# Two-tensor forms for VectorE's 128x4 passes, a wait ahead of three input loads and new instruction lists in a gated cross-attention and quantised feed-forward kernel

## The chip, the cores and the metric

The kernel runs on one core of one Trainium2 chip. Its time is the device time of one launch in microseconds (us), the median of the runs shown. The core has five engines that run their own instruction lists and wait for each other by semaphores: TensorE (PE; its weight loads are PEld), VectorE (DVE), ScalarE (ACT), GpSimd (POOL) and SyncE (SP), which here only issues DMA transfers. ScalarE issues DMA transfers too, at the head of its list.

## The reference, cut to what matters

```python
x = x + tanh(g_xattn) * xattn(layernorm(x), ctx)        # x: 4 x 512 x 256, ctx: 4 x 64 x 256, 16 heads of 16
x = x + tanh(g_ffn) * ffn(layernorm(x))

def xattn(q, k, v):                                     # k = v = ctx
    qh, kh, vh = (q @ Wq.T + bq), (k @ Wk.T + bk), (v @ Wv.T + bv)
    return softmax(qh @ kh.T / 4) @ vh @ Wo.T + bo      # by head

def ffn(x):                                             # 256 -> 1024 -> 256
    h = bit_linear(x, w1)
    h = silu(depthwise_conv1d(h, conv_w, 3 taps) + conv_b)
    return bit_linear(h, w2)

def bit_linear(x, w):                                   # rows of x to 8 bits, w to -1, 0, 1
    s = 127 / max(max_abs(x, by row), 1e-5);  xq = round(x * s) / s
    t = 1 / max(mean_abs(w), 1e-5);           wq = clip(round(w * t), -1, 1) / t
    return xq @ wq.T
```

The norm is over the 256 columns, with 1e-5 added to the variance.

## The kernel before, in words

The four batches of 512 rows pass through one software pipeline. A batch stands in SBUF as four tiles of 128 rows, so each per-row number (mean, root, step) of a batch is a block of 128x4. The stages of batch b are:

- `statistics(b)` and `mean_variance(b)` on VectorE (L676 to L686): statistics by row, then two short passes, `var` = variance + 1e-5 (L685) and `minus_mean` (L686). GpSimd takes the root (`root`, L1378). `norm(b)` runs on VectorE for batch 0, on ScalarE for batch 1 (it then needs `shift`, the negated mean times the root), on GpSimd for 2 and 3.
- TensorE turns the normed rows (`turn_xn`), projects q, computes `scores` once for the row maxima (`row_max`, L720, VectorE) and a second time turned (`scores_t`), minus the maxima; ScalarE takes `exponentials`; TensorE does `values` (L358) and `denominators` (L369), and `project_o` (L397). `residual1` on VectorE adds x.
- `statistics2`, `mean_variance2`, `root2` and `norm2` repeat the norm on the new x. `scale1(b)` on VectorE finds the row maxima of 128x4 (L768) and makes the step (L774), its reciprocal (L777) and the factor back (L780). GpSimd quantises (`quantise1`), TensorE turns and multiplies in eight chunks (`hidden`, L436), and VectorE multiplies each chunk by the factor (`dequantise`, L790).
- The convolution of batches 0 to 2 is half on TensorE (`convolve`, L445) and half on ScalarE and GpSimd (`tap` on ScalarE, `add_left` and `add_right` on GpSimd, L1433 and L1440). Batch 3 is all on TensorE, its second half in two halves of 256 columns. ScalarE takes `silu`.
- VectorE takes the maxima of the hidden rows (`hidden_max_whole`, L812, 4.4 us), `scale2(b)` makes step (L833), reciprocal (L836) and factor (L837), and `quantise_hidden` (L860) writes the quantised tile; TensorE does the product with w2 (`second`, L507). The residual is added by ScalarE and GpSimd for batches 0 to 2, by VectorE for batch 3.

At the start SP issues x of batch 0, the q weights, x of batches 1, 2 and 3 and w2 (L254 to L259), one behind the other and without a wait. ScalarE issues nine more loads (L1202 to L1210): identity, small parameters, context, key weights, a pair indicator, value and output weights, bias rows, w1 and the convolution weights. ScalarE sums the absolute values of w1 and w2 (`weight_sum`, L1058); `weight_scales` turns the sums into scales; w1 is quantised by VectorE, w2 by GpSimd.

The order of the work is written out by hand: each engine has a flat list of calls with the PSUM bank that each uses and the marks that free the bank (from L512 for TensorE, L898 for VectorE, L1211 for ScalarE, L1462 for GpSimd). An engine does its list in order, so an instruction that waits holds all behind it.

Of the kernel before, what the change touches and what calls it, by code (L numbers as in the profile page):

```python
# [12 lines left out]
P = 128  # L13
# [4 lines left out]
T = N // P  # L18
# [33 lines left out]
SPLIT = 3  # L52

# [33 lines left out]
def build(nc, x, ctx_t, attn_w, w1_t, w2_t, conv_d, small, rows, ident, pair_ind, out):  # L87
# [3 lines left out]
    with ExitStack() as es:  # L91
# [29 lines left out]
        minus_half = sb("minus_half", [P, 1])  # L121

# [54 lines left out]

        staged = hid[:, 1].rearrange("p q n i -> p (q n i)")
# [24 lines left out]
        var_ready, rstd_ready = signal("var_ready", 2), signal("rstd_ready")  # L203
# [14 lines left out]
        var2_ready, rstd2_ready = signal("var2_ready", 2), signal("rstd2_ready")  # L218
# [14 lines left out]
        hq_ready = signal("hq_ready", T)  # L233
# [34 lines left out]
        def _(pe):  # L268
# [204 lines left out]
            def spread_scale2_half(b, a, bank, *free):  # L473
# [16 lines left out]
            def spread_scale2(b, bank, *free):  # L490
# [3 lines left out]
                for k in range(T):  # L494
                    last = nc.tensor.transpose(ps[:, bank, k * P:(k + 1) * P],
# [3 lines left out]
            def second(b, h, bank, *free):  # L499
# [4 lines left out]
                for k in (2 * h, 2 * h + 1):  # L504
                    pe.wait_ge(*hq_ready(b, k))
# [47 lines left out]
            project_q(3, 0, 1, mx_ready(1, 2))
            turn_max(1, 5, xT_ready(3, 1))
            project_o(0, 0, 4, oT_ready(0, 0))
            scores_t(1, 0, 6, mx_ready(1, 3))
            scores_t(1, 1, 2, mx_ready(2, 0))
            scores_t(1, 2, 4, x1_ready(0, 0), neg_ready(1))
            project_o(0, 1, 0, oT_ready(0, 1))
            values(1, 0, 6, p_ready(1, 0))  # L560
            denominators(1, 0, 7, p_ready(1, 0))
# [483 lines left out]
        def _(act):  # L1045
# [102 lines left out]
            def own_hid(b):  # L1148
# [4 lines left out]
                if b >= 2:  # L1153
                    act.wait_ge(*hq_ready(b - 2, T - 1))
# [417 lines left out]
```

## Time and profile before

| what | us |
| --- | --- |
| runs of the kernel before: median (lowest to highest) | 168.42 (167.06 to 169.79) |
| the profiled execution | 169.36 |
| span of its trace | 167.2 |

The rows below come from that one profiled execution. Its time is 2.16 us more than its span and 0.94 us more than the median. In a row "x4" is a count of instructions; "[1.69 <-DMA row<-rows]" is the time that the engine stood idle before it and what ended that.

### The profile page before, as it was taken

How to read it: one execution, taken by the hardware profiler on the slowest of the kernel's cores; microseconds unless marked ns; L12 is line 12 of the kernel's file. 1: busy time of each engine (PE TensorE's matmuls, PEld its weight loads, DVE VectorE, ACT ScalarE, POOL GpSimd, SP SyncE). 2: the span in 40 equal slices, each digit the busy share in tenths (PEclk: the TensorE clock that was granted, in tenths of full speed). 3: DMA queues.
4: the chain of work that ended last, by engine and by line, in shares of the span. 5: the costliest groups of instructions: out<-in, count | busy, mean ns of one | idle time of the engine just before them, and what ended most of it. 6: DMA issues, size and time to landing. Idle time of an engine off the chain costs nothing.

```text
span 167.2 us, 3548 instructions
## 1 busy us (share of the span) xinstructions
PE 143.8 (86%) x1314; PEld 79.1 (47%) x1324; DVE 135.2 (81%) x240; ACT 112.3 (67%) x176; POOL 88.3 (53%) x88
## 2 busy tenths in 40 slices
PE   7839979999799999999999796999565999984792
PEld 3238435424565336652576242568333353743461
DVE  6455999961953669995837999999999969989993
ACT  0304598779616488899999997999498586652220
POOL 0204899999910542398370089882979943200330
PEclk9996999999999999999999999999998799999999
DMA  4999800000000000000000000000030000110024
GB/s 134 269 386 395 339 6 0 4 0 0 0 0 2 4 0 0 0 0 4 4 2 0 4 0 2 0 6 0 0 125 0 4 4 0 67 67 0 3 79 169
DMA packets 5919, 8.68 MB, mean 52 GB/s; under 512 B 528, under 2 KB 4880, under 8 KB 5648
## 3 DMA queue, kind: packets, MB, share of 16 engines
q1 hardware_dynamic: 4608, 5.51, 9.6%
q10 hardware_dynamic: 1296, 2.97, 4.7%
q8 instruction: 10, 0.16, 0.4%
q14 instruction: 5, 0.04, 0.1%
HBM read 6.38 MB, written 2.10 MB: 51 GB/s over the span
## 4 chain that ended last, share of the span: by engine, by line
PE 29%; DVE 24%; ACT 24%; issue 15%; DMA 5%; ACTq 1%; DVEq 0%
ACT hid L1181 6%; DMA w_attn<-attn_w 5%; PE ps L445 5%; DVE u L790 4%; DVE mx L720 4%; ACT probs L1120 3%; PE ps L311 3%; DVE hid_q L860 3%; DVE hmax L812 3%; PE ps L348 3%; PE ps L507 2%; ACT side L1169 2%; ACT xn L1079 2%; PE ps L397 2%; DVE top L768 2%
## 5 line engine op out<-in xcount | busy, mean ns | idle before, releaser
L790 DVE TENSOR_TENSOR u<-ps,deq_b 128x512 f32<-128x512 f32 x32 | 20.2, 679 | 4.1 <-PE ps L436 3.6
L1433 POOL TENSOR_TENSOR hid<-hid,side 128x512 f32<-128x512 f32 x12 | 15.6, 1305 | 8.8 <-ACT side L1166 8.8
L720 DVE TENSOR_REDUCE mx<-ps 128x16 f32<-128x1024 f32 x16 | 18.8, 1212 | 1.4 <-PE ps L321 1.4
L445 PE MATMUL ps<-u,conv_w 32*32 32x512 f32 (+1 forms) x576 | 18.5, 544 | 0.9 <-ACT hid L1188 0.7
L1120 ACT ACTIVATE probs<-ps 128x1024 f32<-128x1024 f32 x16 | 15.4, 1029 | 5.6 <-PE ps L348 5.5
L1445 POOL TENSOR_TENSOR x_s<-x_s,grown 128x512 f32<-128x512 f32 x6 | 7.6, 1277 | 21.1 <-ACT grown L1198 21.1
L860 DVE TENSOR_TENSOR hid_q<-hid,ps 128x1024 f16<-128x1024 f32 x16 | 18.6, 1215 | 0.0
L436 PE MATMUL ps<-xqT,w1q 128*128 128x512 bf16 x57 | 15.3, 397 | 3.6 <-ACT xqT L1139 2.9
L1440 POOL TENSOR_TENSOR hid<-hid,side 128x512 f32<-128x512 f32 x12 | 15.5, 1305 | 4.2 <-ACT side L1169 3.8
L507 PE MATMUL ps<-w2q,hid_q 128*128 128x256 f16 x128 | 15.6, 273 | 1.3 <-DVE hid_q L860 1.3
L311 PE MATMUL ps<-xT,w_attn 128*128 128x512 f32 x32 | 15.0, 601 | 0.9 <-DVE mx L720 0.9
L1404 POOL TENSOR_TENSOR rstd<-var,minus_half 128x4 f32<-128x4 f32 x4 | 4.1, 1023 | 21.8 <-DVE minus_mean L762 21.8
L397 PE MATMUL ps<-w_attn,oT 128*128 128x256 f32 x64 | 14.9, 384 | 0.1
L507 PEld LDWEIGHTS ps<-w2q,hid_q 128*128 128x128 f16 x128 | 11.9, 98 | 5.4 <-issue 1.7
L397 PEld LDWEIGHTS ps<-w_attn,oT 128*128 128x128 f32 x64 | 11.8, 190 | 3.4 <-issue 1.6
L812 DVE TENSOR_REDUCE hmax<-hid 128x512 f32<-128x4096 f32 x3 | 13.2, 4409 | 0.2 <-ACT hid L1181 0.2
L445 PEld LDWEIGHTS ps<-u,conv_w 32*32 32x32 f32 x576 | 8.5, 105 | 8.9 <-issue 5.0
L1181 ACT ACTIVATE hid<-ps,par 128x512 f32<-128x512 f32 x16 | 10.3, 731 | 2.8 <-PE ps L445 2.7
L1161 ACT ACTIVATE hid<-u,par 128x512 f32<-128x512 f32 x12 | 9.5, 788 | 3.4 <-DVE u L790 3.4
L743 DVE SCALAR_TENSOR_TENSOR x_s<-ps,tg,x_s 128x512 f32<-128x512 f32 x8 | 5.9, 748 | 6.9 <-PE ps L397 6.8
L436 PEld LDWEIGHTS ps<-xqT,w1q 128*128 128x128 bf16 x64 | 5.9, 99 | 11.5 <-ACT xqT L1139 3.9
L1376 POOL TENSOR_TENSOR kbd<-kT,par 128x1024 f32<-128x1024 f32 x4 | 7.6, 1907 | 6.2 <-ACT kT L1052 6.2
(125 smaller groups left out, 307.2 us busy)
## 6 DMA issues: line engine op xcount, KB each, us to landing
x_s<-x SPq DMA_DIRECT2D x4, 512.0 KB, 12.2
out<-x_s SPq DMA_DIRECT2D x6, 256.0 KB, 2.1
hid<-w_t SPq DMA_DIRECT2D x1, 1024.0 KB, 18.4
hid<-w_t ACTq DMA_DIRECT2D x1, 1024.0 KB, 12.3
w_attn<-attn_w ACTq DMA_DIRECT2D x1, 512.0 KB, 10.0
out<-x_s SPq DMA_DIRECT2D x4, 128.0 KB, 1.8
conv_w<-conv_d ACTq DMA_DIRECT2D x1, 384.0 KB, 13.1
w_attn<-attn_w SPq DMA_DIRECT2D x1, 256.0 KB, 5.7
```

Of the source, the lines that this page charges most:

```text
L311: last = nc.tensor.matmul(ps[:, bank, :], w_attn[:, 0, c, m * P:(m + 1) * P], xT[:, c, :], start=(c == 0), stop=(c == DC - 1))
L397: last = nc.tensor.matmul(ps[:, bank, k % 2 * D:(k % 2 + 1) * D], oT[:, c, k * P:(k + 1) * P], w_attn[:, 3, c, :], start=(c == 0), stop=(c ...
L436: last = nc.tensor.matmul(ps[:, bank, :], w, xqT[:, b % 2, c, :], start=(c == 0), stop=(c == DC - 1))
L445: last = nc.tensor.matmul(ps[ROWS * g:ROWS * g + ROWS, banks[s], first:first + n], conv_w[rg, 4 * q + s, tap, :], u[rg, 4 * q + s, first + ...
L507: last = nc.tensor.matmul(ps[:, bank, k % 2 * D:(k % 2 + 1) * D], hid_q[:, f, k * P:(k + 1) * P], w2q[:, f, :], start=(f == 0), stop=(f == ...
L720: nc.vector.tensor_reduce(mx[:, b % 2, k, 0:HEADS], ps[:, bank:bank + 2, :].rearrange("p c (h k) -> p (c h) k", k=KEYS), AX.X, ALU.max).th ...
L790: nc.vector.tensor_tensor(u[:, f, 1:N + 1], ps[:, bank, :], deq1_b[:, b % 2, :], ALU.mult).then_inc(u_ready.sem, 1)
L812: nc.vector.tensor_reduce(hmax[:], hid[:, b % 2, 0:FP].rearrange("p q n i -> p n q i"), AX.XY, ALU.max, apply_absolute_value=True).then_in ...
L860: nc.vector.tensor_tensor(hid_q[:, :, tile].rearrange("p (q i) n -> p q i n", i=2), hid[:, b % 2, 0:FP, tile, :].rearrange("p q n i -> p q ...
L1120: nc.scalar.activation(probs[:, r], ps[:, bank:bank + 2, :], ACT.Exp, scale=SCORE_SCALE).then_inc(p_ready.sem, 1)
L1181: nc.scalar.activation(dst, src, ACT.Silu, bias=par[:, CB + f:CB + f + 1]).then_inc(hid_ready.sem, 1)
L1433: nc.gpsimd.tensor_tensor(dst, dst, side[:, m % TMPS, 0, :], ALU.add).then_inc(left_ready.sem, 1)
```

## The change

Three things change.

1. The 128x4 passes (and the 128x2 ones of batch 3) that had a number or a column as a scalar now have it as a second tensor, broadcast from a column in SBUF. Four columns are set for it at the start. `minus_mean` is computed only for the batches that ScalarE normalises; VectorE's and GpSimd's norm subtract the mean itself. GpSimd's root now waits for `var` alone.
2. SP waits for the key weights ahead of x of batch 1.
3. All four lists are written anew. Code for a variant in which GpSimd quantises one hidden tile is added, for the batches in TURNED, which is empty.

```diff
+TURNED = frozenset()
...
-                nc.vector.tensor_scalar(var[:, b], mv[:, b, :, 1], LN_EPS, None, ALU.add).then_inc(var_ready.sem, 1)
-                nc.vector.tensor_scalar(minus_mean[:, b], mv[:, b, :, 0], -1.0, None,
-                                        ALU.mult).then_inc(var_ready.sem, 1)
+                nc.vector.tensor_tensor(var[:, b], mv[:, b, :, 1], eps[:].to_broadcast([P, T]),
+                                        ALU.add).then_inc(var_ready.sem, 1)
+                if b in SCALED:
+                    nc.vector.tensor_tensor(minus_mean[:, b], mv[:, b, :, 0], minus_one[:].to_broadcast([P, T]),
+                                            ALU.mult).then_inc(mean_ready.sem, 1)
...
-                nc.vector.tensor_scalar(step1[:, a], top1[:, a], CLIP, 1.0 / QMAX, ALU.max,
-                                        ALU.mult).then_inc(step1_ready.sem, 1)
+                nc.vector.scalar_tensor_tensor(out=step1[:, a], in0=top1[:, a], scalar=CLIP,
+                                               in1=step_of[:, 0:1].to_broadcast([P, T]), op0=ALU.max,
+                                               op1=ALU.mult).then_inc(step1_ready.sem, 1)
...
-                nc.vector.tensor_scalar(deq1[:, a], step1[:, a], wmean[:, 0:1], None,
+                nc.vector.tensor_tensor(deq1[:, a], step1[:, a], wmean[:, 0:1].to_broadcast([P, T]),
                                         ALU.mult).then_inc(scale1_ready.sem, 1)
...
+            nc.vector.memset(eps[:], LN_EPS).then_inc(zeroed, 1)
+            nc.vector.memset(minus_one[:], -1.0).then_inc(zeroed, 1)
+            nc.vector.memset(step_of[:, 0:1], 1.0 / QMAX).then_inc(zeroed, 1)
+            nc.vector.memset(step_of[:, 1:2], 1.0 / (QMAX * F16_STEP)).then_inc(zeroed, 1)
...
             sp.dma_start(w_attn[:, 0], attn_w[:, 0]).then_inc(wq_in, 16)
+
+            sp.wait_ge(wk_in, 16)
             sp.dma_start(x_s[:, 1], x_v[1]).then_inc(x_ins[1], 16)
...
                 if b >= 2:
-                    act.wait_ge(*hq_ready(b - 2, T - 1))
+                    act.wait_ge(*hid_taken(b - 2, T - 2))
+                    act.wait_ge(*hid_taken(b - 2, T - 1))
...
             root(0)
             spread_keys(0)
+            spread_keys(1)
+            residual_base(0)
             root(1)
-            residual_base(0)
+            root(2)
+            root(3)
             residual_base(1)
-            root(2)
-            spread_keys(1)
```

`scale2`, `scale2_of_half` and `mean_variance2` change as `scale1` and `mean_variance` do. ScalarE's `take_q(0, 0)`, `weight_sum(0)`, `take_q(0, 1)`, `norm(1)`, `weight_sum(1)`, `take_xT(1)` now stand in this order; before it was `norm(1)`, both `take_q(0)`, both `take_xT(1)`, both `weight_sum`.

On VectorE, before the weights of the feed-forward are scaled, the list before reads (stat and mv are the statistics of a batch, mx its row maxima, wmean the weights' mean):

```order
L707 TENSOR_TENSOR vbd<-ps,row 64x2x8x16 x4
L676 BN_STATS stat<-x_s 128x6 x4
L682 BN_AGGR mv<-stat 128x2 x4
L685 TENSOR_SCALAR var<-mv 128x4
L686 TENSOR_SCALAR minus_mean<-mv 128x4
L720 TENSOR_REDUCE mx<-ps 128x16 x4
L676 BN_STATS stat<-x_s 128x6 x4
L877 TENSOR_SCALAR wmean<-ps 128x2
L881 RECIPROCAL wscale<-wmean 128x2
L882 TENSOR_SCALAR wdeq<-wmean,tg 128x1
L682 BN_AGGR mv<-stat 128x2 x4
```

The changed list reads at the same place:

```order
L726 TENSOR_TENSOR vbd<-ps,row 64x2x8x16 x4
L693 BN_STATS stat<-x_s 128x6 x8
L699 BN_AGGR mv<-stat 128x2 x4
L702 TENSOR_TENSOR var<-mv,eps 128x4
L699 BN_AGGR mv<-stat 128x2 x4
L702 TENSOR_TENSOR var<-mv,eps 128x4
L739 TENSOR_REDUCE mx<-ps 128x16 x4
L900 TENSOR_SCALAR wmean<-ps 128x2
```

The statistics of batch 3 (the second half of the x8) moved ahead of the four row maxima of batch 0.

On TensorE, around the output projection of batch 0 (w_attn<-oT) and the turned scores of batch 1 (neg_max with ind, then qT with kbd), the list before reads:

```order
L397 MATMUL ps<-w_attn,oT 128x256 x4
L344 MATMUL ps<-neg_max,ind 128x512 x2
L348 MATMUL ps<-qT,kbd 128x512 x2
L344 MATMUL ps<-neg_max,ind 128x512 x2
L348 MATMUL ps<-qT,kbd 128x512 x2
L344 MATMUL ps<-neg_max,ind 128x512 x2
L348 MATMUL ps<-qT,kbd 128x512 x2
L397 MATMUL ps<-w_attn,oT 128x256 x4
L358 MATMUL ps<-probs,vbd 32x512 x4
L369 MATMUL ps<-probs,ones_den 32x512 x4
L344 MATMUL ps<-neg_max,ind 128x512 x2
L348 MATMUL ps<-qT,kbd 128x512 x2
```

The changed list reads there:

```order
L412 MATMUL ps<-w_attn,oT 128x256 x8
L359 MATMUL ps<-neg_max,ind 128x512 x2
L363 MATMUL ps<-qT,kbd 128x512 x2
L359 MATMUL ps<-neg_max,ind 128x512 x2
L363 MATMUL ps<-qT,kbd 128x512 x2
L359 MATMUL ps<-neg_max,ind 128x512 x2
L363 MATMUL ps<-qT,kbd 128x512 x2
L359 MATMUL ps<-neg_max,ind 128x512 x2
L363 MATMUL ps<-qT,kbd 128x512 x2
L326 MATMUL ps<-xT,w_attn 128x512 x2
L384 MATMUL ps<-probs,ones_den 32x512 x4
L373 MATMUL ps<-probs,vbd 32x512 x4
```

The two halves of the projection stand together, the four turned scores behind them, and values and denominators of batch 1 after all four.

On TensorE near the end, around the hidden chunks of batch 3 (xqT with w1q; two of the x10 before the first of them belong to it too), the convolutions (u with conv_w) and the product with w2 (w2q with hid_q), the list before reads:

```order
L445 MATMUL ps<-u,conv_w 32x512 x48
L507 MATMUL ps<-w2q,hid_q 128x256 x16
L436 MATMUL ps<-xqT,w1q 128x512 x10
L445 MATMUL ps<-u,conv_w 32x512 x48
L436 MATMUL ps<-xqT,w1q 128x512 x2
L507 MATMUL ps<-w2q,hid_q 128x256 x16
```

The changed list reads there:

```order
L460 MATMUL ps<-u,conv_w 32x512 x48
L451 MATMUL ps<-xqT,w1q 128x512 x16
L460 MATMUL ps<-u,conv_w 32x512 x48
L460 MATMUL ps<-u,conv_w 32x256 x48
L524 MATMUL ps<-w2q,hid_q 128x256 x16
L503 MATMUL ps<-idf,hmax 128x128 x4
```

All eight chunks of batch 3 follow the convolution of batch 2 directly, and the product with w2 of batch 1 comes after the first half convolution of batch 3.

## Rows read from the trace of the kernel before

**Rows 1.** The page: busy us, share of the span and instructions of each engine.

```profile
PE 143.8 (86%) x1314; PEld 79.1 (47%) x1324; DVE 135.2 (81%) x240; ACT 112.3 (67%) x176; POOL 88.3 (53%) x88
```

**Rows 2.** Windows of 10 us: busy us of each engine, TensorE's clock, DMA share, GB/s.

```profile
10.00:20.00 10.00, 9.00 (x31) 6.67 (x32) 6.62 (x18) 3.42 (x7) 4.56 (x4) 0.83 1.03 395
...
70.00:80.00 10.00, 9.76 (x74) 4.37 (x75) 7.33 (x17) 10.00 (x16) 9.04 (x9) 1.00 0.01 2
...
90.00:100.00 10.00, 9.05 (x66) 3.66 (x70) 9.63 (x18) 9.97 (x14) 3.25 (x6) 1.00 0.01 2
...
150.00:160.00 10.00, 6.05 (x47) 4.17 (x46) 9.86 (x16) 2.73 (x8) 1.27 (x1) 1.00 0.07 26
```

**Rows 3.** The chain that ended last: start us, us on it, what.

```profile
2.14 8.72 DMA w_attn<-attn_w
...
20.95 2.28 DVE var L685
...
53.96 1.00 PE ps L358 x8
...
55.81 0.32 PE ps L344 x2
...
57.96 1.36 ACT xn L1079 x3
```

**Rows 4.** Short VectorE passes by line: ns shortest/median/longest, first and last start.

```profile
L685 DVE TENSOR_SCALAR var<-mv x4: 170/568/2283, 6.9 to 30.0; 128x4 f32<-128x4 f32 x4
...
L774 DVE TENSOR_SCALAR step<-top x4: 171/498/953, 61.3 to 123.3; 128x4 f32<-128x4 f32 x4
...
L780 DVE TENSOR_SCALAR deq<-step,wmean x4: 199/200/1120, 61.6 to 124.4; 128x4 f32<-128x4 f32 x4
...
L833 DVE TENSOR_SCALAR step<-top x3: 170/320/323, 98.6 to 147.5; 128x4 f32<-128x4 f32 x3
...
L837 DVE TENSOR_SCALAR deq<-step,wdeq x3: 200/327/409, 99.0 to 147.8; 128x4 f32<-128x4 f32 x3
```

**Rows 5.** Timelines of GpSimd and VectorE: start us, us, engine, line, what, count.

```profile
18.51 4.70 POOL L1399 TENSOR_TENSOR x_s<-x_s,bo_g 128x1024 f32<-128x1024 f32 x2
...
101.37 1.30 POOL L1440 TENSOR_TENSOR hid<-hid,side 128x512 f32<-128x512 f32 x1
...
101.87 0.82 DVE L774 TENSOR_SCALAR step<-top 128x4 f32<-128x4 f32 x1
102.73 0.18 DVE L777 RECIPROCAL qscale<-step 128x4 f32<-128x4 f32 x1
102.83 1.12 DVE L780 TENSOR_SCALAR deq<-step,wmean 128x4 f32<-128x4 f32 x1
```

**Rows 6.** Timelines of VectorE, ScalarE and SP, and one DMA issue (us to landing).

```profile
5.08 1.41 DVE L676 BATCH_NORM_STATS2 stat<-x_s 128x6 f32<-128x256 f32 x4 [0.87 <-DMA x_s<-x]
...
11.45 1.41 DVE L676 BATCH_NORM_STATS2 stat<-x_s 128x6 f32<-128x256 f32 x4 [1.66 <-DMA x_s<-x]
...
14.54 2.09 DVE L714 TENSOR_SCALAR bo_g<-row,tg 128x256 f32<-128x256 f32 x1 [1.69 <-DMA row<-rows]
...
24.57 1.91 ACT L1058 ACTIVATE w2q<-hid 128x2048 f16<-128x2048 f32 x1
...
59.93 1.25 ACT L1093 ACTIVATE qT<-ps,par 128x512 f32<-128x512 f32 x2
...
3.49 4.02 SPq L259 DMA_DIRECT2D hid<-w_t  x1
...
hid<-w_t SPq DMA_DIRECT2D x1, 1024.0 KB, 18.4
```

**Rows 7.** Timeline of VectorE in batch 3: start us, us, what, [idle before, releaser].

```profile
134.52 1.29 DVE L790 TENSOR_TENSOR u<-ps,deq_b 128x512 f32<-128x512 f32 x2 [0.41 <-PE ps L445]
...
136.70 3.08 DVE L790 TENSOR_TENSOR u<-ps,deq_b 128x512 f32<-128x512 f32 x5 [0.90 <-PE ps L436]
...
148.79 1.75 DVE L821 TENSOR_REDUCE hmax<-hid 128x256 f32<-128x1536 f32 x1 [0.77 <-ACT hid L1188]
```

More of the change, by code:

```diff
@@ L477, in spread_scale2_half @@
                 for k in (2 * a, 2 * a + 1):
-                    last = nc.tensor.transpose(ps[:, bank, k * P:(k + 1) * P],
+                    at = bank + (b in TURNED and k == T - 1)
+                    last = nc.tensor.transpose(ps[:, at, k * P:(k + 1) * P],
                                                qscale2[:, b % 2, k:k + 1].to_broadcast([P, P]), idf[:])
@@ L494, in spread_scale2 @@
                 for k in range(T):
-                    last = nc.tensor.transpose(ps[:, bank, k * P:(k + 1) * P],
+                    at = bank + (b in TURNED and k == T - 1)
+                    last = nc.tensor.transpose(ps[:, at, k * P:(k + 1) * P],
                                                qscale2[:, b % 2, k:k + 1].to_broadcast([P, P]), idf[:])
@@ L553, in _ @@
[L553 to L556, printed above, removed]
-            scores_t(1, 1, 2, mx_ready(2, 0))
[L558 to L561, printed above, removed]
-            scores_t(1, 3, 2, p_ready(1, 1))
-            scores(2, 1, 4, p_ready(1, 2))
@@ new lines, in _ @@
+            scores_t(0, 2, 6, mx_ready(1, 0))
+            scores_t(0, 3, 4, p_ready(0, 0))
+            denominators(0, 0, 0, p_ready(0, 1))
+            turn_xn(3, 0, 1, p_ready(0, 1))
+            turn_xn(3, 1, 6, p_ready(0, 2))
+            denominators(0, 1, 0)
+            scores(1, 1, 4, p_ready(0, 3))
+            scores(1, 2, 2, qT_ready(2, 1))
+            turn_den(0, 7, p_ready(0, 2))
+            scores(1, 3, 0, den_ready(0), xT_ready(3, 0))
+            values(0, 0, 6, xT_ready(3, 1))
@@ new lines, in _ @@
+            scores_t(1, 3, 4, x1_ready(0, 1))
+            project_q(3, 0, 0, p_ready(1, 0))
+            denominators(1, 0, 1, p_ready(1, 0))
+            values(1, 0, 2, p_ready(1, 1))
+            denominators(1, 1, 1)
+            values(1, 1, 3, p_ready(1, 1))
+            scores(2, 2, 6, p_ready(1, 2))
+            turn_den(1, 4, p_ready(1, 3))
+            project_q(3, 1, 5, p_ready(1, 3))
+            spread_deq1(0, 4, rden_ready(1))
+            spread_rden(1, 0, 0, qT_ready(3, 0))
+            scores(2, 3, 2, o_ready(1, 1))
@@ new lines, in _ @@
+            project_o(1, 1, 6, u_ready(0, 1))
+            scores_t(2, 0, 0, u_ready(0, 3))
+            scores_t(2, 1, 4, mx_ready(3, 1))
+            scores_t(2, 2, 2, mx_ready(3, 2))
+            scores_t(2, 3, 6, x1_ready(1, 1))
+            hidden(0, 4, 0, p_ready(2, 0))
+            hidden(0, 5, 1, p_ready(2, 0))
+            hidden(0, 6, 4, p_ready(2, 1))
+            hidden(0, 7, 5, p_ready(2, 1))
+            denominators(2, 0, 0, u_ready(0, 4))
+            values(2, 0, 1, u_ready(0, 5))
@@ new lines, in _ @@
+            denominators(3, 0, 0, p_ready(3, 1))
+            values(3, 0, 1, p_ready(3, 1))
+            denominators(3, 1, 0)
+            hidden(1, 5, 6, p_ready(3, 2))
+            hidden(1, 6, 7, p_ready(3, 2))
+            spread_deq1(2, 1, o_ready(3, 0))
+            turn_den(3, 0, den_ready(3))
+            hidden(1, 7, 4, u_ready(1, 3))
+            turn_hmax(0, 5, u_ready(1, 4))
+            values(3, 1, 2, p_ready(3, 3))
+            turn_xq(2, 3, p_ready(3, 3))
+            spread_rden(3, 0, 6, u_ready(1, 5))
```

676 lines of the change are left out of this document (334 added, 342 removed).

## The prediction

> **What bounds the kernel now.** I read the page first: TensorE is busy for 143.8 us of the span and VectorE for 135.2, 86% and 81% [rows 1]. Shares of a whole span hide stages, so next come windows of 10 us. At 70 to 80 us ScalarE has no gap (10.00) and TensorE hardly one (9.76), while VectorE has 7.33; at 90 to 100 us ScalarE (9.97) and VectorE (9.63) are full; at 150 to 160 us VectorE alone is (9.86), with TensorE at 6.05 [rows 2]. So the front goes by TensorE and the loads, the middle by ScalarE, the rest by VectorE.
>
> The chain of waits then shows where that path holds something that is not work. It begins with the key weights, 8.72 us in the DMA queues. At 20.95 a VectorE pass over 128x4 numbers takes 2.28 us. At 53.96 to 55.81 TensorE does values and denominators of batch 1 before the last scores of that batch, and ScalarE's norm2 of batch 0 starts at 57.96 only [rows 3].
>
> The instructions by line say what those short passes cost. A tensor_scalar of 128x4 takes 170 to 200 ns at its shortest, yet 2283 ns (L685), 953 (L774) or 1120 (L780) at its longest [rows 4]. With the count and the median (for four, shortest plus twice the median plus longest is the sum) the excess over the shortest is 2.9 us on L685, 1.4 on L774, 0.9 on L780, 0.3 on L833 and 0.3 on L837. On the last four the passes that wait start at 98 us or later, as those at 101.87 and 102.83 do [rows 5]: 3.0 us (unrounded) where VectorE is full. The timeline shows the cause: the pass at 20.95 ends at 23.23, GpSimd's two additions at 23.21; the pass at 101.87 ends at 102.69, GpSimd's addition at 102.67. The reciprocal of the same size, from 102.73 on, takes 0.18 us beside the next addition; the tensor_scalar at 102.83 takes 1.12 [rows 5]. So these passes wait for GpSimd's instruction to end, and a reciprocal does not.
>
> **The change part by part.** *Two tensors for a scalar.* Twenty-nine passes keep their size and get a second SBUF tensor (a broadcast column) for the constant. No row shows a VectorE instruction with two SBUF tensors. Bounds from the nearest rows: as the reciprocal, 0.18 us and no wait, so the late 3.0 us go; or as the tensor_scalar, so nothing goes, and another alignment with GpSimd may add as much as it takes. I take no wait: what sets the reciprocal apart from the pass right behind it is the kind of instruction, and the kind is what changes. Term: −3.0 us; bounds −3.0 to 0. L685's 2.9 us belong to the front, below.
>
> The Trainium skill speaks against this. Its page "SBUF — State Buffer", section "Who interferes with whom", says that a VectorE instruction with two SBUF inputs contends with a GpSimd instruction that reads SBUF, and that whoever comes second is blocked until the first has finished. By that rule this term is 0 instead of −3.0. The tensor_scalar rows agree with the page's lock; for two SBUF tensors no run here shows it yet.
>
> *The negated means* stay for the batches that ScalarE normalises and go for five of eight. Late in the run two are gone; their starts cost VectorE some 0.05 us each. Term −0.1. Four more memsets run before x arrives at 5.08, beside VectorE's wait of 0.87 us [rows 6]: nothing. The second wait in own_hid names an event earlier than the one it already waits for: nothing. The code for turned tiles is dead, since TURNED is empty.
>
> *SP's wait on the key weights.* Behind it stand x of batches 1, 2, 3 and w2. The keys landed at 2.14 + 8.72 = 10.86. The first x, 512 KB, was in at 5.08, so it took 5.1 us at most; the key weights, half as large, can then land between 2.14 + 5.08 = 7.2 and 10.9. I take 9, and TensorE starts 1.9 us sooner. Batch 1 lands at about 9 + 5.1 = 14.1 instead of 11.45, 2.6 us later [rows 3, 6]. It is covered: VectorE stood 1.69 us for the bias rows just after, which now come earlier, and the 2.1 us of waiting in the pass at 20.95 have no cause left where var no longer meets an addition [rows 3, 6]. If that cover fails, the 2.6 us are lost.
>
> *The new lists, front and middle.* Statistics of batch 3 move ahead of the first row maxima, the weight sum of w2 ahead of batch 1's xT copies. That sum takes 1.91 us [rows 6] and was behind them: up to 1.9 us against the change on TensorE, with the early keys (1.9) on the other side. What decides is later: both output projections of batch 0 now precede all four scores_t of batch 1, and values and denominators come after them, so the last exponentials, and behind them norm2(0), come up to 55.81 − 53.96 = 1.85 us sooner, less one q copy put ahead of norm2(0), half of 1.25 [rows 3, 6]. Net 1.2 from this. Keys and weight sum about cancel, but part of the sum may hide behind batch 1's turn, so I take −1.5 at ScalarE's first taps. Bounds: +0.7 (the sum costs its 1.9, the keys bring nothing, the reorder 1.2) and −3.1 (keys 1.9 and reorder 1.2, the sum hidden). ScalarE is full from there to 100 us and does the same work, so it carries this to VectorE's full stretch.
>
> *The new lists, late.* In batch 3 VectorE waits 0.41 us at 134.52 and 0.90 at 136.70, both for TensorE, which does the second product of batch 1 and the convolution ahead of hidden chunks, and 0.77 at 148.79 for half a convolution [rows 7]. Now all eight hidden products follow the convolution of batch 2 directly, and VectorE's quantisation of batch 1 covers that convolution. Bounds −2.1 to 0; I take −0.5, since chunks in a row need eight free banks. What is late next is VectorE itself: reductions, products and quantisations stay.
>
> Sum: −1.5 − 3.0 − 0.1 − 0.5 = −5.1. The profiled execution took 169.36 us, so 164.3; it is 0.94 above the median of the runs, 168.42. On that scale: **163.3 us**. Best ends: −3.1 − 3.0 − 0.1 − 2.1 = −8.3, 160.1. Worst of this case: +0.7 − 3.0 − 0.1 = −2.4, 166.0.
>
> **Rivals.** *A: the passes wait as before.* For: every 128x4 pass with a scalar waits, and GpSimd's work is the same. Against: the reciprocal. Then the late 3.0 us stay. In front, root(1) now stands behind residual_base(0), so var(1) can meet that addition, 4.70 / 2 = 2.35 us [rows 5]; half of it takes the front term from −1.5 to −0.3. Sum −0.3 − 0.1 − 0.5 = −0.9: 167.5. The rule of the Trainium skill's page would give this time. It is the case in which the change does not do what its words say.
>
> *B: no waits, but new ones of other engines.* The lists were drawn for durations that the chip need not keep; the front and late terms come to 0 or slightly against: −3.1 + 0.7 = −2.4, 166.0. For: ScalarE and TensorE are as full as VectorE at 70 to 100 us, so freed VectorE time may become idle time.
>
> *C, slower: w2 lands late.* Its 1 MB landed at 3.49 + 18.4 = 21.9 [rows 6] and is the last of 2.5 MB that SP now issues after 9 us. Its sum on ScalarE holds batch 1's xT copies, and these TensorE. Behind the key weights 4.8 MB are left in both queues by the tiles' shapes; at the 395 GB/s of 10 to 20 us [rows 2] that is 12.2 us, 21.2, and costs nothing. From some 22.5 on each us costs one. At 200 GB/s it would be 33: +10.5, less 5.1, so +5.4, 173.8. It ends slower from a landing at 27.6 on. Against: the row shows that rate held over ten microseconds with both queues at work, and ScalarE's queue has enough to keep it so while SP waits.
>
> **How the numbers follow.** Forecast 0.44, A 0.36, B 0.14, C 0.06. About 2% (3.4 us) is what a measurement can tell, so faster means under 165.05. The forecast is under that in about 0.38 of its 0.44, A and B together in 0.07, so faster 0.45; slower is C, 0.05 of its 0.06; within 2% 0.50. Range: 161.0, just above the end where every best bound holds at once, to 168.6, where A's front and late terms are gone too (−0.1, 168.3) with 0.3 for the spread of runs; C and a little of both ends are left out. The likeliest case's own range is 160.1 to 166.0.
>
> **What would show it.** Right: var, step and deq passes of 0.17 to 0.2 us each beside GpSimd's additions; keys on TensorE at about 9; norm2 of batch 0 on ScalarE starting before 57; no wait of VectorE before batch 3's chunks. Wrong: a 128x4 pass that ends with a GpSimd instruction (A), VectorE gaps at 70 to 120 us larger than before (B), ScalarE waiting for w2 past 22.5 (C).

## The result, and the profile after

The changed kernel takes 178.76 us (median of 4 runs, 178.65 to 179.28) against 168.47 for the kernel before in the same session (167.06 to 169.79): a ratio of 1.0647, 95% interval 1.0577 to 1.0716. It is slower by some 10 us; 163.3 was forecast. The profiled execution took 179.28 us, its span is 177.2. A ratio, here and below, is formed from the executions outside a slower state that some of them fall into, so it is not the quotient of the two medians.

The page of the changed kernel begins with the busy time of each engine, as in [rows 1]:

```profile
PE 144.2 (81%) x1316; PEld 81.8 (46%) x1324; DVE 130.3 (74%) x239; ACT 112.2 (63%) x176; POOL 98.9 (56%) x88
```

VectorE works 4.9 us less than before, ScalarE and TensorE the same, and GpSimd 10.6 us more, with the same 88 instructions. So one question is which of GpSimd's instructions got longer. The other comes from the windows of the changed kernel (columns as in [rows 2]):

```profile
10.00:20.00 10.00, 8.19 (x33) 4.78 (x32) 3.61 (x10) 4.95 (x8) 5.61 (x3) 1.00 1.03 379
20.00:30.00 10.00, 3.60 (x13) 2.53 (x14) 9.77 (x28) 5.14 (x8) 6.13 (x7) 0.58 0.03 11
```

The kernel before has this in the second of these windows:

```profile
20.00:30.00 10.00, 8.64 (x37) 4.53 (x37) 9.83 (x24) 9.11 (x15) 9.74 (x9) 1.00 0.04 15
```

From 10 to 20 us VectorE does 3.61 us of work where it did 6.62 [rows 2], and from 20 to 30 us TensorE does 3.60 us where it did 8.64, with a granted clock of 0.58 instead of 1.00. The chain of waits of the changed kernel names two suspects (columns as in [rows 3]):

```profile
2.13 6.85 DMA w_attn<-attn_w
9.00 7.34 DMA x_s<-x
...
31.12 6.25 POOL xn L1428 x3
...
41.62 4.83 POOL xn L1428 x4
...
103.22 4.84 POOL xn L1453 x4
```

The chain of before went from the key weights to VectorE's `var` [rows 3]; now it goes by the load of x of batch 1, which takes 7.34 us behind SP's wait, and then by GpSimd's norm, which it did not touch before. By line (ns shortest/median/longest, first and last start), that norm in the changed kernel, norm of the first kind and norm2:

```profile
L1428 POOL TENSOR_SCALAR xn<-x_s,mv,rstd x8: 1214/1218/2886, 29.9 to 45.2; 128x256 f32<-128x256 f32 x8
...
L1453 POOL TENSOR_SCALAR xn<-x_s,mv,rstd x8: 1217/1222/1227, 103.2 to 133.3; 128x256 f32<-128x256 f32 x8
```

and the same two in the kernel before:

```profile
L1392 POOL TENSOR_SCALAR xn<-x_s,minus_mean,rstd x8: 552/557/560, 26.3 to 40.0; 128x256 f32<-128x256 f32 x8
...
L1416 POOL TENSOR_SCALAR xn<-x_s,minus_mean,rstd x8: 552/554/558, 97.8 to 119.1; 128x256 f32<-128x256 f32 x8
```

Size, type and count are the same; a pass takes 1.22 us instead of 0.55. Sixteen passes make 16 x 0.66 = 10.6 us, all that GpSimd works more. What differs is the text of the instruction: `subtract` of the mean in place of `add` of the negated one.

The timeline of the changed kernel (columns as in [rows 5], idle time and its releaser in brackets) shows what became of SP's wait and of the two-tensor passes:

```profile
16.36 1.41 DVE L693 BATCH_NORM_STATS2 stat<-x_s 128x6 f32<-128x256 f32 x4 [6.54 <-DMA x_s<-x]
...
18.34 2.20 DVE L702 TENSOR_TENSOR var<-mv,eps 128x4 f32<-128x4 f32 x1
...
25.86 0.16 DVE L702 TENSOR_TENSOR var<-mv,eps 128x4 f32<-128x4 f32 x1
...
82.54 1.32 DVE L779 TENSOR_TENSOR var<-mv,eps 128x4 f32<-128x4 f32 x1
...
145.06 4.87 DVE L811 TENSOR_TENSOR u<-ps,deq_b 128x512 f32<-128x512 f32 x8
...
18.16 2.36 POOL L1435 TENSOR_TENSOR x_s<-x_s,bo_g 128x1024 f32<-128x1024 f32 x1 [2.36 <-DVE bo_g L733]
...
25.61 1.98 POOL L1415 TENSOR_TENSOR rstd<-var,minus_half 128x4 f32<-128x4 f32 x2 [3.62 <-DVE var L702]
...
82.55 1.30 POOL L1477 TENSOR_TENSOR hid<-hid,side 128x512 f32<-128x512 f32 x1
...
27.42 1.94 PE L316 MATMUL ps<-idf,xn 128*128 128x128 f32 x8 [3.52 <-DVE mx L739]
...
30.03 6.23 PE L326 MATMUL ps<-xT,w_attn 128*128 128x512 f32 x8 [0.46 <-ACT xT L1114]
```

VectorE stands 6.54 us for x of batch 1. Its `var` then takes 2.20 us and ends at 20.54, GpSimd's addition at 20.52; another takes 1.32 and ends at 83.86, GpSimd's addition at 83.85. So the two-tensor form waits as the scalar form did. TensorE stands 3.52 us for the first row maxima of batch 0, and batch 1's projection of q behind that takes 6.23 us, at a mean granted clock of 0.59 (30.0 to 36.3 us). And the one gain that was forecast for the end is there: eight hidden chunks of batch 3 in a row, from 145.06 on, with no wait in front of them [rows 7].

### The profile page after: what moved, and what is told of

Its sections match the earlier page's. It is cut to its first block, busy times and chain, and to the rows that moved or that the text cites. A ratio compares the mean times of both kernels' runs of the same rounds, so it can differ in the third digit from the quotient of the medians.

```text
span 177.2 us, 3551 instructions
## 1 busy us (share of the span) xinstructions
PE 144.2 (81%) x1316; PEld 81.8 (46%) x1324; DVE 130.3 (74%) x239; ACT 112.2 (63%) x176; POOL 98.9 (56%) x88
## 4 chain that ended last, share of the span: by engine, by line
PE 35%; POOL 18%; DVE 16%; issue 16%; DMA 8%; ACT 3%; ACTq 1%; DVEq 0%; POOLq 0%
PE ps L460 8%; POOL xn L1428 7%; PE ps L412 5%; POOL xn L1453 5%; DVE hid_q L883 4%; DMA x_s<-x 4%; DMA w_attn<-attn_w 4%; PE ps L451 3%; PE ps L373 3%; PE ps L336 3%; DVE stat L693 2%; PE ps L524 2%; DVE top L788 2%; PE ps L326 2%; DVE u L811 2%
## 5 line engine op out<-in xcount | busy, mean ns | idle before, releaser
L460 PE MATMUL ps<-u,conv_w 32*32 32x512 f32 (+1 forms) x576 | 17.7, 528 | 0.3 <-DVE u L811 0.3
L326 PE MATMUL ps<-xT,w_attn 128*128 128x512 f32 x32 | 17.4, 687 | 0.6 <-ACT xT L1114 0.5
L336 PE MATMUL ps<-kbd,qT 128*128 128x512 bf16 x29 | 9.0, 412 | 6.0 <-DVE vbd L726 2.7
L788 DVE TENSOR_REDUCE top<-xn 128x4 f32<-128x1024 f32 x4 | 4.9, 1220 | 10.7 <-ACT xn L1106 6.7
L1428 POOL TENSOR_SCALAR xn<-x_s,mv,rstd 128x256 f32<-128x256 f32 x8 | 12.3, 1546 | 0.0
L1462 POOL TENSOR_SCALAR xq<-xn,qscale 128x256 f32<-128x256 f32 x16 | 7.4, 477 | 7.2 <-DVE deq L801 7.2
## 6 DMA issues: line engine op xcount, KB each, us to landing
hid<-w_t SPq DMA_DIRECT2D x1, 1024.0 KB, 11.2
```

What stands on the lines that cost most here:

```text
L326: last = nc.tensor.matmul(ps[:, bank, :], w_attn[:, 0, c, m * P:(m + 1) * P], xT[:, c, :], start=(c == 0), stop=(c == DC - 1))
L460: last = nc.tensor.matmul(ps[ROWS * g:ROWS * g + ROWS, banks[s], first:first + n], conv_w[rg, 4 * q + s, tap, :], u[rg, 4 * q + s, first + ...
L1428: last = nc.gpsimd.tensor_scalar(xn[:, k, :], x_s[:, b, k, :], mv[:, b, k, 0:1], rstd[:, b, k:k + 1], ALU.subtract, ALU.mult)
```

## The experiments

Twelve kernels were run, each against the kernel before in the same session; its median there was 169.42, 168.97, 169.45 and 169.29 in the four sessions. b_mix has one run, the others 4 to 12.

### The change taken apart

**a_add**: the changed kernel, but GpSimd's norm adds the negated mean again (which VectorE then makes for all batches).

```diff
-    nc.gpsimd.tensor_scalar(xn[:, k, :], x_s[:, b, k, :], mv[:, b, k, 0:1], rstd[:, b, k:k + 1], ALU.subtract, ALU.mult)
+    nc.gpsimd.tensor_scalar(xn[:, k, :], x_s[:, b, k, :], minus_mean[:, b, k:k + 1], rstd[:, b, k:k + 1], ALU.add, ALU.mult)
...
```

> The changed kernel with GpSimd's norm passes (batches 2 and 3, both norms) adding the negated mean again in place of subtracting the mean; VectorE makes the negated mean for those batches too. Theory G (the subtracting form is what costs): the 16 passes of 128x256 fall from 1.22 to 0.55 us, 2.65 us per norm, and of the four norms' 10.6 us some 8 leave the path: about 171. Rival W (the late loads cost it all): passes may shorten, the time stays above 176. Rival L (the lists are bad): above 176 too.

**a_early**: the changed kernel without SP's wait.

```diff
-            sp.wait_ge(wk_in, 16)
```

> The changed kernel without SP's wait on the key weights. Theory W: batch 1's x lands near 11.5 instead of 16.4, the first row maxima start near 22 to 23 instead of 26, TensorE's clock keeps its upper level from 17 to 31 us, and the time falls by 4 to 6 us, to about 174. Theory G alone: at most 1 us less, since GpSimd's slow norm of batch 2 sets the pace behind it.

**a_both**: both edits.

```diff
-            sp.wait_ge(wk_in, 16)
...
-    ... mv[:, b, k, 0:1], rstd[:, b, k:k + 1], ALU.subtract, ALU.mult)
+    ... minus_mean[:, b, k:k + 1], rstd[:, b, k:k + 1], ALU.add, ALU.mult)
```

> The changed kernel with both undone: no wait in SP, GpSimd adds the negated mean. What is left of the change is the two-tensor passes and the lists. Theories G and W together: 164 to 167, what the prediction and its rival A gave for these two parts. Rival L: 172 or more.

**a_lists**: as a_both, and VectorE's short passes in the scalar form of before, so that of the whole change the new lists alone are left.

```diff
-    nc.vector.tensor_tensor(var[:, b], mv[:, b, :, 1], eps[:].to_broadcast([P, T]), ALU.add)
+    nc.vector.tensor_scalar(var[:, b], mv[:, b, :, 1], LN_EPS, None, ALU.add)
...
```

> As the kernel with both undone, and VectorE's short passes written with a scalar again, so that only the lists are left of the change. If two-tensor passes wait for GpSimd as passes with a scalar do (the pass at 18.34 of the changed kernel took 2.20 us and ended with GpSimd's addition), it is within 1 us of the kernel with both undone, and the passes' longest times are alike. If they wait less, it is 2 to 3 us slower.

| kernel | median us | ratio to before (95%) |
| --- | --- | --- |
| a_add | 172.28 | 1.021 (1.0141 to 1.0279) |
| a_early | 175.92 | 1.0405 (1.0358 to 1.0453) |
| a_both | 168.93 | 0.9972 (0.9933 to 1.0012) |
| a_lists | 168.93 | 0.9998 (0.996 to 1.0037) |

The two causes add up. The subtracting norm costs 175.92 − 168.93 = 7.0 us (a_early against a_both), SP's wait 172.28 − 168.93 = 3.35 us (a_add against a_both); together 10.3, and the changed kernel is some 10 above the kernel before. Taken out of the changed kernel's 178.76, which is of another session, they are 6.5 and 2.8. How the norm gets onto the path shows on TensorE in a_early, which turns batch 2's normed rows only after this wait,

```profile
34.55 1.09 PE L315 MATMUL ps<-idf,xn 128*128 128x128 f32 x8 [2.38 <-POOL xn L1427]
```

while in a_both the same matmuls start at 31.82 without one.

Two expectations were missed, and a_add came 1.3 us above its 171. a_early was to come to about 174 with TensorE's clock up from 17 to 31 us; it took 175.92, and from 20 to 30 us the granted clock was 0.83. a_both was to take 164 to 167, or 172 and more if the lists were bad; 168.93 is neither: the lists neither gain nor lose by an amount that shows. What is left of the change, the two-tensor passes and all four lists, is worth nothing that these runs can tell, and of that the two-tensor form alone again nothing: a_both and a_lists have the same median, and the intervals of their ratios overlap from 0.9960 to 1.0012. The rows by line of `var` in a_both,

```profile
L702 DVE TENSOR_TENSOR var<-mv,eps x4: 161/161/1461, 7.3 to 22.7; 128x4 f32<-128x4 f32 x4
```

and in a_lists,

```profile
L702 DVE TENSOR_SCALAR var<-mv x4: 170/170/1469, 7.1 to 22.9; 128x4 f32<-128x4 f32 x4
```

are one experiment of its own: same place in the list, same work of GpSimd, and both forms wait 1.30 us over their shortest. This is what the Trainium skill says in "SBUF — State Buffer", section "Who interferes with whom", of instructions with two SBUF inputs; the measurement agrees with it, and rival A's mechanism was right. One row above does not fit it: at 25.86 a `var` with two tensors took its 0.16 us while GpSimd's 128x4 roots ran from 25.61 to 27.59. The waits whose rows are shown here ended with longer passes of GpSimd.

### Which part of the norm's edit is slow, and is it the lists

**b_sub**: the kernel before with the subtracting norm alone (the edit of a_add the other way round).

```diff
-    nc.gpsimd.tensor_scalar(xn[:, k, :], ..., minus_mean[:, b, k:k + 1], ..., ALU.add, ALU.mult)
+    nc.gpsimd.tensor_scalar(xn[:, k, :], ..., mv[:, b, k, 0:1], ..., ALU.subtract, ALU.mult)
...
```

> The kernel before (old lists, scalar passes, no wait of SP) with one edit: GpSimd's norm subtracts the mean column instead of adding the negated one. Theory G (the subtracting form is slow on GpSimd whatever the lists): its 16 passes take 1.22 us each instead of 0.55, 2.7 us more for each of four norms, and the kernel takes 173 to 176, as the same edit was worth 6.5 to 7.0 us in the new lists. Rival: the pass is only slow beside VectorE's work of the new lists; then 0.55 us stays and 169. Second rival: the passes are slow, but GpSimd has room in the old lists: under 171.

It took 180.30 us, ratio 1.067 (1.0576 to 1.0763): more than the whole change. The old lists are more exposed to it than the new ones, beyond what either theory gave. Sixteen passes of 0.66 us more are 10.6 us, and 180.30 − 168.97 = 11.3 are lost. The chain of waits of b_sub goes by GpSimd's norm in three of its four places (from 25.10, 101.74 and 125.54 us), 3 x 2.65 = 8.0 us of it; where the rest is lost is not shown.

**b_mix**: the kernel before, norm with the new operand and the old operation, norm2 with the old operand and the new operation.

```diff
-    nc.gpsimd.tensor_scalar(xn[:, k, :], ..., minus_mean[:, b, k:k + 1], ..., ALU.add, ALU.mult)
+    nc.gpsimd.tensor_scalar(xn[:, k, :], ..., mv[:, b, k, 0:1], ..., ALU.add, ALU.mult)
...
-    nc.gpsimd.tensor_scalar(xn2[:, k, :], ..., minus_mean2[:, b % 2, k:k + 1], ..., ALU.add, ALU.mult)
+    nc.gpsimd.tensor_scalar(xn2[:, k, :], ..., minus_mean2[:, b % 2, k:k + 1], ..., ALU.subtract, ALU.mult)
```

> The kernel before with GpSimd's norm changed in two ways that each take half of the edit: in norm of batches 2 and 3 it adds the mean column itself (the new operand, the old operation), in norm2 of batches 2 and 3 it subtracts the negated mean (the old operand, the new operation). Both leave the mean with the wrong sign there, which costs no time. Theory S (the operation is the slow thing): the first passes stay at 0.55 us, the second take 1.22, and the kernel takes about 5 more than before. Rival O (the operand, a column of a tile of two columns): the first take 1.22, the second 0.55.

It took 175.22 us in its one run, 5.8 more than the median of before. The rows by line:

```profile
L1392 POOL TENSOR_SCALAR xn<-x_s,mv,rstd x8: 548/560/1515, 25.5 to 39.5; 128x256 f32<-128x256 f32 x8
...
L1416 POOL TENSOR_SCALAR xn<-x_s,minus_mean,rstd x8: 1212/1222/1225, 97.7 to 123.9; 128x256 f32<-128x256 f32 x8
```

Theory S holds: the new operand costs nothing (median 560 ns; the longest, 1515, stood beside VectorE's quantisation of w1), the operation costs 0.66 us a pass. VectorE's own norm of batch 0 underwent the same edit. In the kernel before and in the changed kernel it stands so:

```profile
8.41 1.38 DVE L694 TENSOR_SCALAR xn<-x_s,minus_mean,rstd 128x256 f32<-128x256 f32 x4 [1.24 <-POOL rstd L1380]
...
8.44 1.38 DVE L713 TENSOR_SCALAR xn<-x_s,mv,rstd 128x256 f32<-128x256 f32 x4 [1.25 <-POOL rstd L1415]
```

It is 1.38 us for four passes in both forms, so VectorE pays nothing for `subtract`. Why GpSimd does is not shown.

### SP's wait, and TensorE's clock behind it

**b_wait**: the kernel before with SP's wait alone.

```diff
+            sp.wait_ge(wk_in, 16)
             sp.dma_start(x_s[:, 1], x_v[1]).then_inc(x_ins[1], 16)
```

> The kernel before with SP's wait on the key weights alone. Theory W: keys reach TensorE near 9 instead of 10.9, x of batch 1 lands near 16.4 instead of 11.45, VectorE stands some 6 us ahead of its statistics, and the kernel takes about 172, 3 us more. Rival, the step of the forecast: covered by the idle time for the bias rows and by the pass at 20.95; then 168 to 169.5.

171.29 us, ratio 1.0144 (1.0081 to 1.0208). The row that decides:

```profile
15.78 1.41 DVE L677 BATCH_NORM_STATS2 stat<-x_s 128x6 f32<-128x256 f32 x4 [5.91 <-DMA x_s<-x]
```

Theory W holds, with 2.3 us instead of 3: x of batch 1 arrives 4.3 us later than in [rows 6], and in the old lists too this is covered only in part. VectorE's first row maxima start 1.1 us later (24.40 instead of 23.34), and TensorE waits for batch 1's normed rows:

```profile
21.54 1.97 PE L302 MATMUL ps<-idf,xn 128*128 128x128 f32 x8 [4.99 <-ACT xn L1071]
```

From 20 to 30 us its granted clock is 0.66, where the kernel before has 1.00.

**a_fill**: a_both, with matmuls of ones that nobody reads where TensorE stands in the front.

```diff
...
+            fill(1, 7)
             scores(0, 0, 6)
...
             scores(0, 2, 2, qT_ready(0, 0), v_ready(0, 3))
+            fill(2, 4, qT_ready(0, 1))
             scores(0, 3, 4, qT_ready(0, 1))
```

> The changed kernel with GpSimd adding the negated mean and without SP's wait, and three matmuls of ones that nobody reads (some 0.9 us each) where TensorE stands at 18.6 and at 22.1. Theory C (the front of the new lists loses its gain to the half clock that follows that idle time): batch 1's q projection takes 3.6 us instead of 5.4, and the time falls by 1 to 1.7, to 167.2 to 167.9. Rival: the projection gets shorter, but the path goes by VectorE or GpSimd there, and the time stays at 168.9.

168.66 us, ratio 0.9967 (0.9928 to 1.0007), against 0.9972 for a_both in another session. TensorE's timeline in a_both,

```profile
20.12 1.98 PE L336 MATMUL ps<-kbd,qT 128*128 128x512 bf16 x8 [1.53 <-ACT qT L1120]
24.37 1.06 PE L316 MATMUL ps<-idf,xn 128*128 128x128 f32 x8 [2.27 <-DVE mx L739]
...
26.16 5.38 PE L326 MATMUL ps<-xT,w_attn 128*128 128x512 f32 x8 [0.30 <-ACT xT L1114]
```

and in a_fill:

```profile
26.54 3.70 PE L326 MATMUL ps<-xT,w_attn 128*128 128x512 f32 x8 [0.31 <-ACT xT L1122]
```

The clock half of theory C holds in these two executions: with the idle stretches of 1.53 and 2.27 us filled but for 0.67 and 0.54 the same eight matmuls take 3.70 us instead of 5.38, and from 20 to 30 us the granted clock is 1.00 (0.83 in a_both, with 0.50 from 26.5 to 29.5). Its time half does not hold: 1.7 us saved in these matmuls are 0.5 at the first top of batch 0 on VectorE (59.58 instead of 60.04), and the ratio moves by 0.0005, far inside the interval.

**w_fill**: the same idea on a_add, which keeps SP's wait: 1 matmul ahead of the first scores, 3 ahead of the third, 3 ahead of the fourth.

```diff
+            fill(1, 7)
             scores(0, 0, 6)
...
+            fill(3, 4, qT_ready(0, 1))
             scores(0, 2, 2, qT_ready(0, 0), v_ready(0, 3))
+            fill(3, 4, qT_ready(0, 1))
             scores(0, 3, 4, qT_ready(0, 1))
```

> The changed kernel with GpSimd adding the negated mean, SP's wait kept (172.3 without the fill), and seven matmuls of ones that nobody reads where TensorE stands between 16.3 and 26.7. Theory C (of the 3.4 us that the wait costs, some two are the half clock): batch 1's q projection takes 3.6 us instead of 5.9 and the time falls to 170 to 170.7. Rival (the lateness of x itself costs it, through VectorE's row maxima): the projection gets shorter and the time stays within 0.7 of 172.3.

170.92 us, ratio 1.0117 (1.0042 to 1.0192). This is between the two expectations. The projection still took 5.39 us (5.90 in a_add); TensorE stood another 1.45 us for the row maxima ahead of it. The intervals of w_fill and a_add overlap, so that the fill gained anything is not shown, and how the wait's cost divides between lateness and clock stays open.

### Towards a better kernel

**a_pool**: a_fill with one fill matmul fewer, and the variance plus 1e-5 and the negated means made by GpSimd, ahead of its root.

```diff
-                nc.vector.tensor_tensor(var[:, b], mv[:, b, :, 1], eps[:].to_broadcast([P, T]), ALU.add)
...
-                pool.wait_ge(*var_ready(b))
+                pool.wait_ge(*mv_ready(b))
+                nc.gpsimd.tensor_tensor(var[:, b], mv[:, b, :, 1], eps[:].to_broadcast([P, T]), ALU.add)
...
```

> As the filled kernel (adding norm, no wait of SP, fill of TensorE, one matmul fewer), but the variance plus 1e-5 and the negated means are made by GpSimd ahead of its root, so that VectorE has 8 of the waiting passes fewer, and some 7 of the negated means. Theory V (what VectorE waits for GpSimd in the front holds up its row maxima): the first row maxima start near 21.5 instead of 23.4, and the time is 166.8 to 167.8. Rival: only the pass starts late in the run are saved, some 0.3 us, since the middle goes by ScalarE: 168.2 to 168.7.

168.73 us, ratio 0.9965 (0.9931 to 0.9999). The row maxima did come early:

```profile
20.89 4.62 DVE L741 TENSOR_REDUCE mx<-ps 128x16 f32<-128x1024 f32 x4
...
25.18 0.38 PE L309 MATMUL ps<-wtot,ones 128*128 128x2 f32 x2 [0.80 <-ACT w2q L1081]
26.14 5.40 PE L326 MATMUL ps<-xT,w_attn 128*128 128x512 f32 x8 [0.57 <-ACT xT L1110]
```

They start at 20.89 instead of 23.38 in a_fill, and the projection of batch 1 still starts at 26.14: now TensorE stands for the weight sum of w2 (0.80) and for the xT copies behind it on ScalarE (0.57), and the projection takes 5.40 us again, with a granted clock of 0.50 from 26.5 to 29.5 us. No idle stretch of TensorE from 18 to 26 us was longer than 0.80 us here, so the clock can fall without any as long as those of a_both. One matmul of ones fewer than in a_fill stood ahead of it; whether that brought the clock down is not taken apart. Theory V fails on its second half; the rival's time, 168.2 to 168.7, is met to 0.03.

**a_pool2**: a_pool, and GpSimd makes the factors back too (`deq1`, and `deq2` of batches 0 to 2).

```diff
-                nc.vector.tensor_tensor(deq1[:, a], step1[:, a], wmean[:, 0:1].to_broadcast([P, T]), ALU.mult)
...
+                nc.gpsimd.tensor_tensor(deq1[:, b % 2], step1[:, b % 2], wmean[:, 0:1].to_broadcast([P, T]), ALU.mult)
...
```

> As the one before it, and the factors back (step times the weights' mean) of the first product, and of the second product for batches 0 to 2, are made by GpSimd too; one of them waited 1.14 us on VectorE at 104, where VectorE is full. Theory V: 1.5 to 2 us less than the one before it, near 165.5 to 166.5. Rival: the wait moves to the next two-tensor pass behind, and the time falls by under 0.5.

166.93 us (166.39 to 168.07), ratio 0.9889 (0.9836 to 0.9942): the fastest kernel of the study, 1.1% faster than the kernel before. VectorE around 100 us in a_pool,

```profile
100.13 0.18 DVE L794 RECIPROCAL qscale<-step 128x4 f32<-128x4 f32 x1
100.23 1.23 DVE L797 TENSOR_TENSOR deq<-step,wmean 128x4 f32<-128x4 f32 x1
...
104.57 0.18 DVE L854 RECIPROCAL qscale<-step 128x4 f32<-128x4 f32 x1
104.67 1.13 DVE L855 TENSOR_TENSOR deq<-step,wdeq 128x4 f32<-128x4 f32 x1
```

and in a_pool2:

```profile
100.31 0.18 DVE L794 RECIPROCAL qscale<-step 128x4 f32<-128x4 f32 x1
100.40 1.87 DVE L803 TENSOR_TENSOR u<-ps,deq_b 128x512 f32<-128x512 f32 x3
...
104.91 0.18 DVE L850 RECIPROCAL qscale<-step 128x4 f32<-128x4 f32 x1
105.00 1.27 DVE L803 TENSOR_TENSOR u<-ps,deq_b 128x512 f32<-128x512 f32 x2
```

The two passes that waited, 1.23 and 1.13 us, are gone from VectorE; on GpSimd such a pass takes 0.20 us, behind whatever GpSimd is doing. The move is worth 1.8 us against a_pool by the medians of one session (168.73 − 166.93) and 1.3 by the ratios; theory V said 1.5 to 2, though from a lower time of a_pool. In these two executions VectorE gives part of the freed time back at once: it stands 0.68 and 0.31 us for TensorE and reaches the next product, oT, at 106.19 instead of 106.92. Where the rest is gained is not shown.

**a_front**: a_pool2, with the weight sum of w2 behind batch 1's xT copies on ScalarE, the totals behind batch 1's projection on TensorE, and the copy of the quantised w1 behind the first two exponentials.

```diff
-            weight_totals(0, mx_ready(0, 1))
             project_q(1, 0, 1, mx_ready(0, 1))
-            project_q(1, 1, 0, wmean_ready())
+            project_q(1, 1, 0, mx_ready(0, 1))
+            weight_totals(2, mx_ready(0, 2))
...
```

> As the one before it (166.9), with the weight sum of w2 behind batch 1's xT copies on ScalarE, the totals behind batch 1's q projection on TensorE, and the copy of the quantised w1 behind the first two exponentials. Theory F (the front term of the forecast was lost because this sum holds the xT copies, and TensorE, which stands meanwhile, then works at half clock): batch 1's q projection starts near 24.6 instead of 26.4 and takes 3.6 us instead of 5.3, norm2 of batch 0 starts on ScalarE near 55.5 instead of 58.4, and the time falls by 1.5 to 3, to 164 to 165.5. Rival (the middle is set by ScalarE's and VectorE's own lists whenever they begin): the projection is early, and the time stays within 0.7 of 166.9.

168.13 us, ratio 0.9969 (0.992 to 1.0018), in another session than a_pool2 (0.9889, 0.9836 to 0.9942): no gain over it, if anything a loss. Its profiled execution took 169.98. The eight matmuls on the key weights take 3.60 us there instead of 1.97, and the matmuls behind them run some 1.8 us later than in a_pool2, so only waits within it are read:

```profile
31.01 0.16 DVE L890 TENSOR_SCALAR wmean<-ps 128x2 f32<-128x2 f32 x1 [3.66 <-PE ps L309]
...
27.16 3.70 PE L326 MATMUL ps<-xT,w_attn 128*128 128x512 f32 x8 [0.73 <-ACT xT L1104]
...
40.17 0.52 PE L359 MATMUL ps<-neg_max,ind 32*128 32x512 bf16 x4 [2.52 <-DVE mx L741]
```

The projection is at full clock, as theory F said, but this execution's clock had fallen earlier already (0.83 from 10 to 20 us, where a_pool2 has 1.00), so that the edit did it is not shown. VectorE now stands 3.66 us for the totals (0.30 in a_pool2) and quantises w1 that much later, and TensorE stands 2.52 us for the row maxima of batch 1, a wait that a_pool2 does not have. By this one trace the gap moved; it was not closed.

## Why the prediction was wrong, point by point

- **GpSimd's norm.** This is the step that failed worst, by not being a step: the change's description said that VectorE's and GpSimd's norm subtract the mean itself, and the part on the negated means priced only what VectorE saves (−0.1). The edited instruction on GpSimd got no row, no bound and no rival. It cost 7.0 us in the new lists. No row showed GpSimd subtracting, so the nearest rows, 16 passes of 0.55 us with `add`, were no price for it but the start of a range; a guess of twice the duration, 8.9 us more, would have made a slower rival.
- **SP's wait.** It was put at nothing, since the later x was "covered", with 2.6 us lost if not. The keys landed at 9.00, as forecast; x of batch 1 at 16.36 instead of 14.1. The forecast gave it the 5.1 us of the first x. While that one landed the queues moved some 0.8 MB (192 GB/s from 0.7 to 5.1 us, changed kernel); behind the wait, with three more loads issued right after it, it took 7.34 us, in which they moved some 2.8 MB (390 GB/s from 9.0 to 16.3). The cover failed too: the pass at 20.95 was to lose its wait, and `var` took 2.20 us. The wait cost 2.3 (old lists) to 3.35 us (new lists). Not named at all was TensorE's answer: it stood 1.53, 2.74 and 3.52 us, its granted clock was 0.58 from 20 to 30 us, and batch 1's projection took 6.23 us instead of 3.67.
- **Two tensors for a scalar, −3.0.** Measured 0, the other end of the bound. What set the reciprocal apart was not that the scalar operand was missing. Rival A, and with it the rule of the Trainium skill's page, had it right; the chance of 0.36 was too small for a mechanism that a stated rule backed against a single pair of rows.
- **New lists in front, −1.5.** Measured 0: norm2 of batch 0 starts on ScalarE at 57.96 in [rows 3] and at 57.93 in a_both, which leaves out SP's wait and so the 1.9 us of the early keys; these the forecast set off against the weight sum. The term counted one end of the exchange. ScalarE's timeline in a_both,

```profile
53.48 3.77 ACT L1147 ACTIVATE probs<-ps 128x1024 f32<-128x1024 f32 x4 [4.05 <-PE ps L363]
57.11 0.71 ACT L1120 ACTIVATE qT<-ps,par 128x512 f32<-128x512 f32 x1
57.93 2.07 ACT L1106 ACTIVATE xn<-x_s,shift,rstd 128x256 f32<-128x256 f32 x4
```

  and in the kernel before:

```profile
51.01 2.85 ACT L1120 ACTIVATE probs<-ps 128x1024 f32<-128x1024 f32 x3 [2.33 <-PE ps L348]
...
57.04 1.02 ACT L1120 ACTIVATE probs<-ps 128x1024 f32<-128x1024 f32 x1 [1.44 <-PE ps L348]
```

  The last exponential did lose its wait for values and denominators. But with both output projections ahead of the turned scores, all four exponentials wait for these, start 2.5 us later, and need 3.77 us in a row; with the q copy behind them norm2 starts where it did. On top of it the lower clock took 1.7 us of TensorE's front; a_fill, which got them back there, has norm2 at 57.47, 0.5 us sooner.
- **New lists late, −0.5.** Measured 0.2 at most: from norm2 of batch 0 to the end of the trace it is 109.2 us in the kernel before and 109.1 in a_both. The mechanism was right (145.06 above, no wait), but other waits ate it. Busy time of `deq2` and of the half steps in a_lists (busy us, mean ns of one, idle before),

```profile
L850 DVE TENSOR_SCALAR deq<-step,wdeq 128x4 f32<-128x4 f32 x3 | 1.7, 551 | 0.0
...
L860 DVE TENSOR_SCALAR step<-top 128x2 f32<-128x2 f32 x2 | 0.9, 473 | 0.1
```

  and in the kernel before:

```profile
L837 DVE TENSOR_SCALAR deq<-step,wdeq 128x4 f32<-128x4 f32 x3 | 0.9, 312 | 0.0
...
L848 DVE TENSOR_SCALAR step<-top 128x2 f32<-128x2 f32 x2 | 0.3, 169 | 0.1
```

  1.4 us more, in the stretch in which VectorE is full: the new order meets GpSimd's additions at other passes. This reading is by rows of two profiled executions; no run took it apart.
- **Rival B** held for the lists, as just told; with A's waits it makes the forecast's own 168.3, near the 168.93 of a_both. **Rival C** did not come: w2 was issued at 10.52 and took 11.2 us, so it landed at 21.7, under the 22.5 from which it costs.
- **The range**, 161.0 to 168.6, and the 0.05 for slower missed the result because the only slower case was w2, and because the wait's own price, named as 2.6 us if uncovered, was not carried into the upper end: A's 167.5 and 2.6 make 170.1. Even that leaves out the norm's 7.0.

## What to carry to other kernels

Price every instruction whose operation or operand changes, on the engine that runs it, even where the words of a change treat it as the consequence of saving something elsewhere; an algebraic identity is not one in time. A load that is held back can cost twice when the engine that waits for it feeds TensorE: once in lateness and once in the clock, which was lower behind the wait in both lists here (how the cost divides stayed open). A gap that is closed in one list opens in the next one, so follow the freed time until it reaches an engine that is full. Where short passes of a full engine wait for a neighbour's long ones, another form of the same pass may wait just as long; giving the pass to the neighbour was worth 1.8 us for the factors back and nothing for `var` and the negated means.

## What the runs showed of the hardware

- A GpSimd tensor_scalar over 128x256 numbers in fp32 takes 0.55 us as `add` then `mult` and 1.22 us as `subtract` then `mult`; which column the mean comes from makes no difference (0.56). VectorE shows no such difference: 1.38 us for four passes either way.
- VectorE's 128x4 passes wait for GpSimd's additions in scalar form (1.469 us) and with two tensors (1.461) alike; reductions of 128x1024 from SBUF (1219 to 1221 ns in the changed kernel, two of the four beside an addition) and reciprocals (178 ns) do not, and neither did a two-tensor pass beside GpSimd's 128x4 root (0.16).
- Idle stretches of 1.53 and 2.27 us on TensorE (a_both) were followed by matmuls partly at its lower clock, 5.38 us for what takes 3.70 at the upper one; with these stretches filled but for 0.67 and 0.54 us the clock stayed up (a_fill), and with idle stretches of 0.80 us and less it fell all the same (a_pool).
